# A test-time-training layer with an expert layer on one core: the spread of the inverse's blocks at 384 columns, and transposes and full fp32 products moved next to each other

## What is computed

```python
def step(carry, kvq):
    W, b = carry
    k, v, q = kvq
    pred = W @ k + b
    g = 2.0 / d_h * (pred - v)
    W = W - LR * jnp.outer(g, k)
    b = b - LR * g
    out = W @ q + b
...
x = _layernorm(x + ttt(x), axis=-1)
x = _layernorm(x + ffn(x), axis=-1)
```

## Time and profile before

| | |
|---|---|
| timed runs, median (lowest to highest) | 2440.41 us (2440.23 to 2451.82), 3 runs |
| the profiled execution | 2445.45 us, its span 2443.6 us |
| TensorE busy over the span | 2256.2 us, 92% |
| VectorE, ScalarE, GpSimd busy | 1533.8, 885.3, 1108.9 us |
| chain that ended last | 71% TensorE, 8% DMA, 7% GpSimd, 7% issue, 5% VectorE |

### The profile page before, as it was taken

The page is one execution under the profiler, slowest core; times in us unless marked ns, Lnnn a source line. Parts: engine busy times, 40 slices in busy tenths (PEclk is TensorE's granted clock), DMA queues, the critical chain, the costliest instruction groups (busy, mean ns, idle before and its releaser), DMA issues.

```text
span 2443.6 us, 40067 instructions
## 1 busy us (share of the span) xinstructions
PE 2256.2 (92%) x13154; PEld 1950.1 (80%) x13154; DVE 1533.8 (63%) x3579; ACT 885.3 (36%) x1887; POOL 1108.9 (45%) x1061
## 2 busy tenths in 40 slices
PE   6999999999999999999999999998689999999870
PEld 5888888888888788888888887887478789888750
DVE  5655666555666766566655566764645445887886
ACT  3333333333333333333333333332445445544430
POOL 1333443333343334445554443455463533676776
PEclk9999999999999999999999999999789999999995
DMA  4011111011111001111111111120686866888897
GB/s 160 22 46 38 35 44 44 35 45 43 35 44 44 35 35 40 48 35 44 41 39 40 48 35 35 35 45 27 199 112 152 125 141 190 293 291 267 291 306 232
DMA packets 121174, 233.26 MB, mean 95 GB/s; under 512 B 36944, under 2 KB 37456, under 8 KB 120208
## 3 DMA queue, kind: packets, MB, share of 16 engines
q1 hardware_dynamic: 83680, 157.96, 19.5%
q0 software_dynamic: 26256, 72.71, 12.4%
q10 hardware_dynamic: 11040, 0.04, 0.3%
HBM read 141.11 MB, written 89.53 MB: 94 GB/s over the span
## 4 chain that ended last, share of the span: by engine, by line
PE 71%; DMA 8%; POOL 7%; issue 7%; DVE 5%; ACT 1%; SPq 0%; DVEq 0%; POOLq 0%; ACTq 0%
PE banks L106 20%; PE banks L108 20%; PE banks L107 20%; PE banks L112 7%; DMA b_XN<-x1d,IDX 5%; POOL RG L1791 2%; POOL b_XN L1779 2%; DMA ids<-idt,POS 2%; PE banks L706 1%; PE banks L444 1%; PE banks L543 1%; POOL ids L1712 1%; POOL b_small L1665 1%; DMA S<-in_we 1%; DVE xc L1053 1%
## 5 line engine op out<-in xcount | busy, mean ns | idle before, releaser
L106 PE MATMUL banks<-W 128*128 128x512 f32 (+1 forms) x2040 | 753.5, 369 | 15.8 <-DVE W L1050 15.8
L108 PE MATMUL banks<-W 128*128 128x512 f32 (+1 forms) x2040 | 718.3, 352 | 0.0
L107 PE MATMUL banks<-W 128*128 128x512 f32 (+1 forms) x2040 | 716.9, 351 | 0.0
L106 PEld LDWEIGHTS banks<-W 128*128 128x128 f32 x2040 | 388.8, 191 | 67.8 <-POOL W L1665 15.0
L108 PEld LDWEIGHTS banks<-W 128*128 128x128 f32 x2040 | 387.4, 190 | 54.3
L107 PEld LDWEIGHTS banks<-W 128*128 128x128 f32 x2040 | 389.1, 191 | 50.9 <-issue 7.2
L1665 POOL TENSOR_TENSOR W<-S,W 128x512 fp32r<-128x512 f32 x256 | 327.4, 1307 | 118.2 <-ACT W L769 118.2
L769 ACT ACTIVATE W<-banks 128x512 fp32r<-128x512 f32 x320 | 191.2, 597 | 519.3 <-DVE banks L1050 241.5
L1665 POOL TENSOR_TENSOR X<-X,B 128x1024 f32<-128x1024 f32 x32 | 78.7, 2460 | 641.0 <-DMA X<-in_x 641.0
L769 ACT ACTIVATE W<-S 128x512 fp32r<-128x512 f32 (+1 forms) x288 | 180.7, 651 | 228.7 <-DVE S L1050 210.7
L1050 DVE TENSOR_TENSOR W<-banks,W 128x512 fp32r<-128x512 f32 x192 | 132.2, 689 | 174.0 <-ACT W L769 174.0
(11 more groups left out here) (152 smaller groups left out, 4476.0 us busy)
## 6 DMA issues: line engine op xcount, KB each, us to landing
ys<-b_Y SPq DMA_DIRECT2D x149, 256.0 KB
XT<-in_xT SPq DMA_DIRECT2D x32, 512.0 KB, 3.6
X<-in_x SPq DMA_DIRECT2D x32, 512.0 KB, 3.5
x1d<-X SPq DMA_DIRECT2D x64, 256.0 KB, 2.2
zd<-X SPq DMA_DIRECT2D x64, 256.0 KB, 2.0
b_Y<-zd SPq DMA_DIRECT2D x64, 256.0 KB, 4.5
out<-b_Y SPq DMA_DIRECT2D x64, 256.0 KB, 4.5
S<-in_we SPq DMA_DIRECT2D x32, 256.0 KB, 5.4
```

The costliest lines, as they stand in the source:

```text
L106: e.matmul(o, ll, rh, start=start, stop=False, skip_group_check=True)
L107: e.matmul(o, lh, rl, start=False, stop=False, skip_group_check=True)
L108: return e.matmul(o, lh, rh, start=False, stop=stop, skip_group_check=True)
```

## The change

It has two parts. `R` no longer holds all 16 columns for all 16 rows of a block: the rows 0 to 7 keep 16 columns, the rows 8 to 15 keep the last 8. So R is 2 x 8 x (16 + 8) = 384 columns wide, VectorE writes it with two instructions, and `spread_blocks` multiplies 384 columns. And pieces change places in the orders, above all on TensorE, so that fp32 instructions stand together: `spread_blocks` goes ahead of `b_part`; `back_x1(t-1,0)` goes behind `up_x1(t-1,1)`, next to `inv_m`; `inv_n(t,1)` goes behind `qs_part(t,0,1)`, next to `k_turn(n,0)`; `inv_n(t,2)` goes behind `k_proj(n,1,1)` and `qs_part(t,1,0)`, next to `k_turn(n,1)`. VectorE and ScalarE follow.

```diff
+HS = BS // 2
+BLK = NB * HS * (BS + HS)
...
+def block_rows(x):
+
+    n = NB * HS * BS
+    return [x[:, 0:n].rearrange("p (i b j) -> p i b j", i=HS, b=NB), x[:, n:BLK].rearrange("p (i b j) -> p i b j", i=HS, b=NB)]
...
-        w.wait_ge(k.s_R, t + 1)
-        mm(e, o, k.cst[:, 2, :], k.R.rearrange("p i b j -> p (i b j)")).then_inc(k.s_Lb, 1)
+        w.wait_ge(k.s_R, 2 * t + 2)
+        mm(e, o[:, 0:BLK], k.cst[:, 2, :], k.R).then_inc(k.s_Lb, 1)
...
         p_part(t, 1)
         if t > 0:
+            up_x1(t - 1, 1)
             back_x1(t - 1, 0)
-            up_x1(t - 1, 1)
         inv_m(t)
...
             inv_t(t, 1)
             if t > 0:
                 down_x1(t - 1, 0)
-            else:
-                qs_part(t, 0, 1)
+            qs_part(t, 0, 1)
             inv_n(t, 1)
-            if t > 0:
-                qs_part(t, 0, 1)
             k_turn(n, 0)
             k_proj(n, 1, 0)
             inv_t(t, 2)
             if t > 0:
                 down_x1(t - 1, 1)
-            else:
-                k_proj(n, 1, 1)
+            k_proj(n, 1, 1)
+            qs_part(t, 1, 0)
             inv_n(t, 2)
-            if t > 0:
-                k_proj(n, 1, 1)
-            qs_part(t, 1, 0)
+            k_turn(n, 1)
             qs_part(t, 1, 1)
-            k_turn(n, 1)
...
         turn_x1(t, 0)
         if more:
+            spread_blocks(n)
             b_part(t, 0)
             b_part(t, 1)
-            spread_blocks(n)
@@ scalar_program @@
         p_part(t, 1)
         if t > 0:
-            back_x1(t - 1, 0)
             up_x1(t - 1, 1)
         inv_m(t)
+        if t > 0:
+            back_x1(t - 1, 0)
@@ vector_program @@
-        tt(k.R, gd.unsqueeze(1).to_broadcast(rows), unit_lr.unsqueeze(2).unsqueeze(3).to_broadcast(rows), ALU.mult).then_inc(k.s_R, 1)
-        w.wait_ge(k.s_R, t + 1)
+        for h, o in enumerate(block_rows(k.R)):
+            rows = [P, HS, NB, (BS, HS)[h]]
+            own = unit_lr[:, h * HS:(h + 1) * HS].unsqueeze(2).unsqueeze(3)
+            tt(o, gd[:, :, h * HS:BS].unsqueeze(1).to_broadcast(rows), own.to_broadcast(rows), ALU.mult).then_inc(k.s_R, 1)
+        w.wait_ge(k.s_R, 2 * t + 2)
...
             if t > 0:
                 down_x1(t - 1, 1)
                 tick()
+            k_proj(n, 1)
+            tick()
             inv_n(t, 2)
-            tick()
-            k_proj(n, 1)
...
             b_part(t, 0)
             tick()
-            b_part(t, 1)
-            tick()
...
         turn_x1(t, 0)
         tick()
+        if more:
+            b_part(t, 1)
+            tick()
```

More of the change, by code:

```diff
@@ L282, in first_memory @@
         k.onesr, k.cst = sb("onesr", [P], F32R), sb("cst", [NCST, P])
-        k.R = k.MM[:].rearrange("p k b n -> p (k b n)").rearrange("p (i b j) -> p i b j", i=BS, b=NB)
+        k.R = k.MM[:].rearrange("p k b n -> p (k b n)")[:, 0:BLK]
         k.xc, k.rw = sb("xc", [NB, BS]), sb("rw", [KC, E])
@@ L1084, in scores @@
         e.tensor_reduce(gd, k.T1[:].rearrange("p b (k j) -> p b j k", k=NBL), AX.X, ALU.add).then_inc(k.s_sc, 1)
-        rows = [P, BS, NB, BS]
         w.wait_ge(k.s_sc, 4 * t + 3)
@@ L1097, in subst @@
     def subst(t):
-        n0, lb = 2 * (BS - 1) * t, at["Lb", t].rearrange("p (i b j) -> p i b j", i=BS, b=NB)
+        n0, (upper, lower) = 2 * (BS - 1) * t, block_rows(at["Lb", t])
         w.wait_ge(k.s_Lb, t + 1)
@@ L1103, in subst @@
         for b in range(NB):
-            stt(k.xc[:, b, 1:BS], lb[:, 0, b, 1:BS], unit[:, 0:1], unit[:, 1:BS], ALU.mult, ALU.add).then_inc(k.s_sub, 1)
+            stt(k.xc[:, b, 1:BS], upper[:, 0, b, 1:BS], unit[:, 0:1], unit[:, 1:BS], ALU.mult, ALU.add).then_inc(k.s_sub, 1)
         yield
@@ L1109, in subst @@
                 w.wait_ge(k.s_sub, n0 + 2 * j + b - 1)
-                stt(rest, lb[:, j, b, j + 1:BS], k.xc[:, b, j:j + 1], rest, ALU.mult, ALU.add).then_inc(k.s_sub, 1)
+                row = upper[:, j, b, j + 1:BS] if j < HS else lower[:, j - HS, b, j + 1 - HS:HS]
+                stt(rest, row, k.xc[:, b, j:j + 1], rest, ALU.mult, ALU.add).then_inc(k.s_sub, 1)
             yield
@@ L1455, in vector_program @@
         if t > 0:
+            logits(t - 1, 1)
+            tick()
             back_x1(t - 1, 0)
-            tick()
-        if t > 0:
-            logits(t - 1, 1)
         for g in k.groups[:-1]:
```

## The result

The changed kernel takes 2454.58 us (median of 17 runs, 2447.81 to 2459.98), the kernel before 2446.68 (median of 17 runs, 2437.19 to 2454.47). The ratio is 1.0039, with a 95% interval of 1.0028 to 1.005: slower, by 7.9 us going by the medians and 9.5 by the ratio, which is under half a percent but clear of the noise, and outside the range of the prediction (2435 to 2451). The miss against the forecast of 2445.5 is 9.1 us. Of it 6.3 us is the base: the sum was laid on the median of three runs, 2440.41, and the median of the 17, which hold these three, is 2446.68. The remaining 3 us or so is a loss larger than the +5 forecast.

A forecast was written before the change was run, and what follows sets the result against it. TensorE was taken to set the pace at 52.66 us a step. A middle step's +0.01 + 0.22 - 0.02 = +0.21 us, over 26 steps, gave about +5 on 2440.4: 2445.5 us, range 2435 to 2451.

The forecast's parts named there:

- the base: Whole program: the +5 us was added to a median of 2440.4 us for the kernel before.
- I take 0 for these three: Steps 1, 15 and 27, where ScalarE loads a table ahead of the SiLU: no change in time.
- The wait: TensorE ahead of the second product of `up_x1`: the wait for `X1l` grows from 0.25 to 0.70 us.
- Two groups fewer, -0.02: fp32 groups on TensorE: two fewer per step save 2 x 0.01 us.
- `inv_n`: Levels 1 and 2 of the inverse: moving them later is free, with 0.8 and 2.4 us left.
- A: Rival, middle steps: the spread's saving comes through, 0.235 us a step, 2435 us in all; chance 0.12.
- B: Rival, fp32 groups on TensorE: leaving fp32 for fp32r costs 0.15 us per group, giving 2427 us; chance 0.04.
- C: Rival, `inv_t(t,2)`: the inverse becomes the last to come, TensorE waits 0.3 us, 2453 us or more; chance 0.05.
- D: Rival, VectorE's addition: TensorE's `p_part` stays the last to come, a step is as long as before, 2440 us; chance 0.17.

The follow-up runs named there:

- third: Changed kernel with the spread put back behind the products with ones on TensorE: 2438.17 us, ratio 1.0013, 52.63 us a middle step.
- fourth: Changed kernel with `back_x1(t-1,0)` put back ahead of `up_x1(t-1,1)` on TensorE, ScalarE and VectorE: 2439.1 us, ratio 1.0014.
- fifth kernel: Changed kernel with VectorE writing `X1l` for b=1 ahead of the second half of `p_part(t,0)`: 2441.06 us against 2446.0, ratio 0.9968.
- first kernel: Kernel before with the 384-column spread alone, in the old order: 2428.72 us against 2435.86, ratio 0.9977.
- second: Changed kernel with the spread back at 512 columns, so the new order alone: 2447.78 us against 2435.86, ratio 1.0056.
- seventh: Kernel before with only the two moves of `inv_n`: 2451.24 us in one run beside a median of 2446.0.
- last kernel: Changed kernel with the router's piece behind the whole substitution and VectorE's old order of bias additions and `X1l`: 2495.2 us against 2493.92, ratio 1.0002.

## Where the prediction was right, and where it was wrong

The prediction was wrong as a whole: 2454.58 us lies above its range. Two terms of its sum failed. The base of 2440.4 us, taken from three runs, was 6.3 us low, and "I take 0 for these three" put the unusual steps at nothing where the profile has 3.8 us. The mechanism that it gave for the middle steps held.

*The wait, right.* `up_x1(.,1)` waits for `X1l`, and the edge that was full is VectorE's. The narrow slot (0.64 against 0.645), the chain of 3.46 us, the missing pause and the place of the new gap are all as worked out. The wait is 0.63 and not 0.70, and a step loses 0.18 us and not 0.21; the gap between the starts in TensorE's timeline is 0.75 us and not 0.8 to 0.9. Taking each move back returned what its term said (the third, fourth and fifth kernel).

*Two groups fewer, -0.02, wrong but small.* They save nothing (52.70 us a step with these moves alone, 52.65 without).

*`inv_n`, right.* No wait appears at the inverse. TensorE's timeline around `inv_t` of level 2, in the changed kernel, shows none:

```profile
977.49 0.60 PE L120 MATMUL banks<-MM,LT 128*128 128x128 f32 x4
977.85 0.48 PE L114 MATMUL banks<-WS,HL 128*128 128x512 f32 x1
```

*Rivals.* A (the saving comes through) fails in this order, and holds in the old one (first kernel). B (leaving fp32 drains) falls with the second and seventh kernels. C (the inverse last) and D (TensorE's `p_part` last) did not happen; the measured time is near C's figure of 2453.5, but for another reason.

*"I take 0 for these three": the first step that failed.* The prediction looked in step 15 at the table load alone. That part held in the order: ScalarE now copies the level's matrix at 857.89, ahead of the load at 858.30, and the wait of 0.95 us is gone. That most of it returns at `inv_n(t,0)` held only in part: 0.54 us with VectorE's old order, 0.41 in the changed kernel's second profile, nothing in its first. What it left out is VectorE, which has the router's work there and decides the step. The new order of the additions and `X1l` shortens one wait and lengthens the next, and the fall of the clock moves to where TensorE has nothing to wait for. That is +1.98 us at steps 14 to 16 and +1.85 at steps 26 to 28, and in step 16 1.1 more where the last scan loses against GpSimd, or 2.7 where the clock falls behind it as well. The text had this clock term, 1.7 us for each unusual step, only in its upper bound of +11, and on the base of 2440.4 even that bound (2451.4) lies below the measured time. Step 1, the third unusual one, can't be read: it varies by 1 us between profiles of the kernel before.

*The base: the second step that failed, and the larger part of the miss.* The sum was laid on 2440.4, the median of three runs, and two of these three are the third and fourth lowest of the 17. Such a draw is chance; the step that failed is taking it as exact, since the range left nothing for it, though the third run was 2451.82 and the profiled execution 2445.45. On 2446.7 the same +5 gives 2451.7 and the range 2441 to 2457, which holds the 2454.58 measured: the difference that is left, 3 us, is about the unusual steps' share.

*Open.* Why the total of the last kernel lies below the sum of its steps, and what costs 0.05 us in the seventh.

## What to carry to other kernels

Time taken off the busiest engine is worth only what its next wait leaves: follow that wait back to the engine that releases it, and see which instruction the new order puts later there. Price the unusual steps separately, with the list of what the releasing engine does in them, since a wait there is paid twice if the clock falls behind it. Take the base from as many runs as the answer needs: here the choice of three runs moved the forecast by 6.3 us, with the whole change worth 8. Here the better version was the narrow spread in the old order with the awaited instruction moved up on VectorE (0.9947).

## What the runs showed of the hardware

A fall of the granted clock to 0.50 for 3.4 us in front of a wait cost nothing (a step of 59.50 us with it and without), and behind one 1.4 to 1.65 us. A small VectorE scan of 0.19 us took 1.28 to 1.30 us in five profiles in which GpSimd's addition had begun 0.16 to 0.17 us earlier, and 0.20 in one in which it had begun 0.15 us earlier. Changing from fp32 to fp32r and back showed no cost: 0.110 and 0.112 us an instruction in groups of four and of ten, and 52.22 and 52.23 us a step in the two orders.
